# Last stage of a decoder: the second expert's down products and sums one slot later, values of two heads in one row strip

## The reference

```python
# cross attention, 16 heads of 8 features, 77 keys
scores = jnp.einsum('bhqd,bhkd->bhqk', Q, K) / math.sqrt(dk)
...
t = jnp.exp(log_t)[..., None]
attn = jax.nn.softmax(qk / (2.0 * t), axis=-1)
out = jnp.einsum('bhqk,bhkd->bhqd', attn, V)
x = x + _linear(out.transpose(0, 2, 1, 3).reshape(b, sq, d), Wo, bo)
# four experts, the best two of four weighted for each token
e0 = jax.nn.silu(x @ sw_w1) * (x @ sw_w3) @ sw_w2
e1 = jax.nn.gelu(sym @ me_c1w + me_c1b, approximate=False) @ me_c2w + me_c2b
...
h2 = _layer_norm(syn + attn, ce_n1g, ce_n1b)
ff = jax.nn.relu(h2 @ ce_f1w + ce_f1b) @ ce_f2w + ce_f2b
e2 = _layer_norm(h2 + ff, ce_n2g, ce_n2b) @ ce_gen_w + ce_gen_b
e3 = jax.nn.gelu(x @ ml_w1 + ml_b1, approximate=False) @ ml_w2 + ml_b2
```

## Time and profile before

| | us |
|---|---|
| median of 3 runs (lowest, highest) | 3040.72 (3040.23, 3042.76) |
| the profiled execution | 3037.89 |
| its span | 3036.1 |
| last stage, from about | 2066 |
| PE busy | 2738.4 |
| DVE busy | 2097.9 |
| ACT busy | 1920.1 |
| POOL busy | 1943.3 |

### The profile page before, as it was taken

The page is one execution under the profiler, slowest core; times in us unless marked ns, Lnnn a source line. Parts: engine busy times, 40 slices in busy tenths (PEclk is TensorE's granted clock), DMA queues, the critical chain, the costliest instruction groups (busy, mean ns, idle before and its releaser), DMA issues. The chain is left out here.

```text
span 3036.1 us, 83028 instructions
## 1 busy us (share of the span) xinstructions
PE 2738.4 (90%) x27974; PEld 2320.1 (76%) x27975; DVE 2097.9 (69%) x4496; ACT 1920.1 (63%) x4300; POOL 1943.3 (64%) x3244
## 2 busy tenths in 40 slices
PE   6999997999999999499997999995899999999996
PEld 5788776888888888388885888883677777777775
DVE  3677655667676766445555999997777878778543
ACT  3566553666666666355553777774878777787762
POOL 4456543456666666416667999984676777867652
PEclk9999997999999999699998999995899999999998
DMA  5566561000000000222222000000000000000000
GB/s 153 169 181 190 170 181 36 2 8 12 14 13 13 12 14 13 71 67 82 81 82 62 1 0 0 0 1 1 1 2 9 5 8 5 5 9 5 8 5 11
DMA packets 204792, 129.08 MB, mean 43 GB/s; under 512 B 13840, under 2 KB 197112, under 8 KB 203896
## 3 DMA queue, kind: packets, MB, share of 16 engines
q1 hardware_dynamic: 196344, 108.80, 12.0%
q0 software_dynamic: 8192, 16.79, 1.9%
HBM read 35.05 MB, written 90.51 MB: 41 GB/s over the span
## 5 line engine op out<-in xcount | busy, mean ns | idle before, releaser
L1552 PE MATMUL a_ps_s<-a_qk,w_ident 128*128 128x256 f32 x1024 | 238.5, 387 | 20.2 <-POOL a_qk L1659 19.1
L1007 POOL TENSOR_TENSOR x_p<-x_p,x_rz 128x1232 f32<-128x1232 f32 x64 | 143.9, 2248 | 165.6 <-DVE x_rz L1116 165.6
L584 DVE TENSOR_REDUCE a_nmax<-a_ps_s 128x4 f32<-128x512 f32 x256 | 164.9, 686 | 113.8 <-PE a_ps_s L373 113.7
L1659 POOL TENSOR_TENSOR a_qk<-a_qkv 128x2048 f32<-128x2048 f32 x64 | 235.6, 3681 | 2.6 <-POOL a_eight L218 1.0
L457 ACT ACTIVATE a_e<-a_ps_s 128x512 f32<-128x512 f32 x256 | 138.9, 595 | 152.8 <-PE a_ps_s L378 152.8
L1552 PEld LDWEIGHTS a_ps_s<-a_qk,w_ident 128*128 128x128 f32 x1024 | 192.0, 193 | 50.4 <-POOL a_qk L1659 22.7
L2374 POOL TENSOR_TENSOR x_sq<-x_e 128x1232 f32<-128x1232 f32 x64 | 143.2, 2238 | 126.2 <-DVE x_t_sq L2533 126.1
L1633 ACT ACTIVATE a_r<-a_o,w_a_rows 128x128 f32<-128x128 f32 x512 | 220.5, 521 | 1.6 <-DVE a_o L1718 1.6
L1387 POOL DMA_INDIRECT f_yg<-f_rows_out,f_index x120 | 114.9, 958 | 152.1 <-DVE f_yo L1467 134.4
L889 ACT ACTIVATE x_uu_hi<-x_ps_u 128x308 fp32r<-128x308 f32 x256 | 101.7, 423 | 106.0 <-PE x_ps_u L752 105.8
L1123 DVE TENSOR_REDUCE x_top<-x_ps_s 128x16 f32<-128x1232 f32 x64 | 91.2, 1424 | 111.2 <-PE x_ps_s L752 111.2
(11 more groups left out here) (626 smaller groups left out, 9742.0 us busy)
## 6 DMA issues: line engine op xcount, KB each, us to landing
f_rows_in<-a_zeros SPq DMA_DIRECT2D x31, 1088.0 KB, 5.4
f_rows_out<-a_zeros SPq DMA_DIRECT2D x31, 1088.0 KB, 8.8
f_xin<-f_rows_in SPq DMA_DIRECT2D x135, 64.0 KB
f_rows_out<-f_yo SPq DMA_DIRECT2D x135, 64.0 KB, 1.6
out<-x SPq DMA_DIRECT2D x16, 256.0 KB, 2.4
f_raw<-in_late_f SPq DMA_DIRECT2D x2, 1408.0 KB, 5.9
w_ctx<-in_ctx SPq DMA_DIRECT2D x1, 2464.0 KB
f_rows_in<-f_xr,f_where POOLq DMA_INDIRECT x128, 2.3
```

Source lines behind the costliest of these rows:

```text
L584: nc.vector.tensor_reduce(nmax[:, u % 2, g, :], ps_s[g][:, :].rearrange("p (t k) -> p t k", t=GROUP), AX.X, ALU.max, negate=True).then_inc ...
L1007: nc.gpsimd.tensor_tensor(wide, wide, rz[:, :].unsqueeze(2).broadcast_to([P, HEADS, K]), ALU.mult).then_inc(p_ready, 1)
L1552: ins = nc.tensor.matmul(ps_s[u % 2][:, 0:HEADS * HEADS], c.ident[:, :], qk[:, u % 2, k, :, :], start=k == 0, stop=k == HD - 1)
L1659: nc.gpsimd.tensor_tensor(qk[:, u % 2, :, :, :], qkv[:, u % UNROLL, 0, :, :].unsqueeze(3).broadcast_to(full), qkv[:, u % UNROLL, 1, :, :]. ...
```

## The change

1. `second` no longer holds b's down products. A new `third` issues them at place 1 of the gates' slot (THIRD = OPEN + 5), ahead of gate 0, and VectorE's `finished("b")` moves to place 1 of that slot. In `sums_of` b stands behind d and ahead of the `up` products. d's down products, one sequence of the tile each, stand at places 1, 4, 6 and 7 of SECOND instead of one at 4, two at 6 and one at 7.
2. v1 is 40 columns wide, zeros with the values in columns 8 to 15 and a one in column 24. Two heads use it with a window of 32 that begins at column 8 or 0, and their products are summed into one strip: rows 0 to 7 and 8 to 15 are the values, rows 16 and 24 the sums of the weights. ps_o then holds 256 columns, oz copies 256, two transposes turn them back, and the scaling is two instructions of 64 values.

```diff
-        v1 = sb("v1", [K, 2, HEADS, STRIP])
+        v1 = sb("v1", [K, 2, HEADS, WIDE])
...
             if (j := tile(t, SECOND)) is not None:
-                order += [("b", j, 0), ("d", j, 0)]
+                order += [("d", j, 0)]
+            if (j := tile(t, THIRD)) is not None:
+                order += [("b", j, 0)]
             if (j := tile(t, GATED)) is not None:
...
+                if n in (1, 4, 6, 7):
+                    downs("d", j, range(4), f["ml_2"], ((1, 4, 6, 7).index(n),))
+
+            def third(j, n):
+
                 if n == 1:
                     downs("b", j, (4, 5), f["c2"], range(T))
-                if n == 4:
-                    downs("d", j, range(4), f["ml_2"], (0,))
-                if n == 6:
-                    downs("d", j, range(4), f["ml_2"], (1, 2))
-                if n == 7:
-                    downs("d", j, range(4), f["ml_2"], (3,))
...
                         j, r = divmod(n, GROUPS)
+                        two, low = divmod(j, PAIR)
                         h = GROUP * r + j
-                        ins = nc.tensor.matmul(ps_o[strip(r), j * P:j * P + P], v1[:, s % 2, h, :], pT[:, h, :],
-                                               start=True, stop=True)
+                        ins = nc.tensor.matmul(ps_o[strip(r), two * P:two * P + P], v1[:, s % 2, h, HD - HD * low:WIDE - HD * low], pT[:, h, :],
+                                               start=low == 0, stop=low == PAIR - 1)
...
-                    for j in range(GROUP):
+                    for j in range(2):
                         ins = nc.tensor.transpose(ps_o[:, j * P:j * P + P], oz[:, j * P:j * P + P], c.ident[:, :])
...
-                    nc.scalar.activation(oz[:, :], ps_o[:, :], ACT.Copy).then_inc(oz_ready, 1)
+                    nc.scalar.activation(oz[:, :], ps_o[:, 0:2 * P], ACT.Copy).then_inc(oz_ready, 1)
...
-            nc.gpsimd.memset(v1[:, :, :, :], 1.0).then_inc(made, 1)
+            nc.gpsimd.memset(v1[:, :, :, :], 0.0).then_inc(pool_made, 1)
+            pool.wait_ge(pool_made, 3)
+            nc.gpsimd.memset(v1[:, :, :, 3 * HD:3 * HD + 1], 1.0).then_inc(made, 1)
...
-                if (j := tile(t, SECOND)) is not None and n == 1:
+                if (j := tile(t, THIRD)) is not None and n == 1:
                     finished("b", 1, j, "c2b")
...
-                    nc.vector.reciprocal(each, z[:, :, :, HD]).then_inc(rz_ready, 1)
+                    nc.vector.reciprocal(rz[:, :, :, :], z[:, :, :, 2 * HD::HD]).then_inc(rz_ready, 1)
...
+                    for n in range(2):
+                        ins = nc.vector.tensor_tensor(out[:, n, :, :, :], z[:, n, :, 0:2 * HD].rearrange("p g (j d) -> p g j d", d=HD),
+                                                      rz[:, n, :, :].unsqueeze(3).broadcast_to([P, GROUPS, PAIR, HD]), ALU.mult)
+                    ins.then_inc(o_ready, 1)
```

More of the change, by code:

```diff
@@ L1811, in cross_and_experts @@
         e, sq = sb("e", [P, 2, HEADS, K]), sb("sq", [P, HEADS, K])
-        v1 = sb("v1", [K, 2, HEADS, STRIP])
+        WIDE, PAIR = HD + STRIP, GROUP // 2
+        v1 = sb("v1", [K, 2, HEADS, WIDE])
         pT = sb("pT", [K, HEADS, P])
-        oz, rz, o = sb("oz", [P, 512]), sb("rz", [P, HEADS]), sb("o", [P, 2, D])
+        oz, rz, o = sb("oz", [P, 2 * P]), sb("rz", [P, PAIR, GROUPS, PAIR]), sb("o", [P, 2, D])
         t_max, t_z, t_sq = (sb(n, [P, 2, GRP, HEADS]) for n in ("t_max", "t_z", "t_sq"))
@@ L1883, in tile @@
             return (t - lag) // T if (t - lag) % T == 0 and 0 <= (t - lag) // T < TILES else None
-        OPENED, GATED, TURNED, MIXED, SECOND, TURNED2, CLOSED = (OPEN + n for n in (0, 1, 2, 3, 4, 6, 7))
+        OPENED, GATED, TURNED, MIXED, SECOND, THIRD, TURNED2, CLOSED = (OPEN + n for n in (0, 1, 2, 3, 4, 5, 6, 7))
         def gated(t):
@@ L2106, in experts @@
                     second(j, n)
+                if (j := tile(t, THIRD)) is not None:
+                    third(j, n)
                 if (j := tile(t, OPENED)) is not None:
@@ L2285, in _ @@
                     act.wait_ge(p_ps, t - PROJECT + 1)
-                    nc.scalar.activation(v1[:, spread % 2, :, 0:HD], ps_v.rearrange("p (h r) -> p h r", r=HD), ACT.Copy).then_inc(v_ready, 1)
+                    nc.scalar.activation(v1[:, spread % 2, :, HD:2 * HD], ps_v.rearrange("p (h r) -> p h r", r=HD), ACT.Copy).then_inc(v_ready, 1)
                 experts(t, 2)
@@ L2543, in _ @@
                     dve.wait_ge(z_ps, s + 1)
-                    z = ps_o[:, :].rearrange("p (j g r) -> p g j r", j=GROUP, g=GROUPS)
-                    each = rz[:, :].rearrange("p (g j) -> p g j", g=GROUPS)
-                    nc.vector.reciprocal(each, z[:, :, :, HD]).then_inc(rz_ready, 1)
+                    z = ps_o[:, 0:2 * P].rearrange("p (n g r) -> p n g r", n=2, g=GROUPS)
+                    nc.vector.reciprocal(rz[:, :, :, :], z[:, :, :, 2 * HD::HD]).then_inc(rz_ready, 1)
                     dve.wait_ge(rz_ready, s + 1)
                     wait(dve, oT_ps, s - 1)
-                    nc.vector.tensor_tensor(o[:, s % 2, :].rearrange("p (g j r) -> p g j r", g=GROUPS, j=GROUP), z[:, :, :, 0:HD],
-                                            each.unsqueeze(3).broadcast_to([P, GROUPS, GROUP, HD]), ALU.mult).then_inc(o_ready, 1)
+                    out = o[:, s % 2, :].rearrange("p (g n j d) -> p n g j d", g=GROUPS, n=2, j=PAIR)
+                    for n in range(2):
+                        ins = nc.vector.tensor_tensor(out[:, n, :, :, :], z[:, n, :, 0:2 * HD].rearrange("p g (j d) -> p g j d", d=HD),
+                                                      rz[:, n, :, :].unsqueeze(3).broadcast_to([P, GROUPS, PAIR, HD]), ALU.mult)
+                    ins.then_inc(o_ready, 1)
                 experts(t, 7)
```

## The result

The changed kernel took 3095.91 us (median of 4 runs, 3090.07 to 3099.68), the kernel before 3040.47 (4 runs, 3036.44 to 3042.76): 1.0183 times as long, 95% interval 1.0166 to 1.0199.

A forecast was written before the change was run, and what follows sets the result against it. VectorE's order in the gates' slot, not TensorE's amount of work, was taken to bound the kernel. 29.7 + 3 + 0.4 + 5.6 = +38.7 on the profiled 3037.9 gave 3076.6, with the median 2.8 above: 3079 us, range 3054 to 3098.

The forecast's parts named there:

- the forecast's own range: 3060 to 3090 us: a period at 2 to 3 us, clock at 0 to 10, end at its bounds; chance 0.70.
- SECOND loses nothing but its tail: SECOND: b's 1.79 us taken away were covered by ScalarE's chain; the router's operations start only 0.6 us earlier.
- The gates' slot: b's products wait for d's sum to free ps_d: stall 2.8 us, transposes of the weights +2.9 us, 0.6 already taken off.
- x: The forecast's new start of the router's operations on VectorE, 2519.80.
- 11 x (2.9 - 0.2) = +29.7: Eleven gates' slots with maximum and subtraction: 2.9 us lost in each, 0.2 given back by the pairing.
- The pairing: Two of four z transposes go; they pay only at the end of the TURNED slot: -0.2 us per four slots.
- The clock: Falls behind the 2.8 us stall cost 1.4 us each; bounds none and all 11, 0 to +15; four taken, +5.6.
- The rival with a fall in every gates' slot: Clock falls in every gates' slot: +15.4 for the clock, +48.5 in all, 3089 us; chance 0.13.
- The one of 2.16 cost nothing: Argument against the clock falling in every gates' slot: behind a 2.16 us stall at 2225.36 the granted clock stayed 1.00.
- The end: Last four slots, without maximum and subtraction: +1, +1, +2 and -1, so +3 us (ends -4 and +11).
- The faster rival: TensorE's amount of work decides: 128 transposes less at 0.11 us are 14.1 us, giving 3026.6; chance 0.07.
- the absorbed one: POOL's normalisation sets the gates' slot's end anyway, hiding TensorE's 2.7 us loss: only +3 and 0.4 stay, 3044 us; chance 0.05.

The follow-up runs named there:

- the kernel with fillers: Changed kernel plus 16 transposes into ps_o, ahead of the value products, where TensorE waits for d's sum in the gates' slot: 1.0104 of before.

## Why the prediction was right, point by point

Predicted 3079.0 in 3054 to 3098, slower at 0.87; measured 3095.91. The mechanism held; two sizes were off, in opposite directions. The measurement lies beyond the forecast's own range (3060 to 3090) and only 2 us inside the wide one: that it is inside at all owes something to luck, since no term stood for the largest error, the clock at the stage's end.

- **SECOND loses nothing but its tail.** The first 1.79 us were covered, as said: o's transpose still waits for ScalarE's v, now 0.98 us where it was 0.21. The way from there to the router's first operation took 7.22 us (2536.98 to 2544.20), before 8.05: 0.8 earlier, forecast 0.6. The difference is ScalarE's copy, 384 ns for 256 columns, so 0.2 less than the 596, in its one place on a chain.
- **The gates' slot.** Stall 2.37 us (said: 2.8); at full clock, in the kernel with fillers, up 0 at x + 7.43 (7.6) and the weights' transposes at x + 9.22 (9.35). From x to them were 5.83 us before, so +3.39, less 0.83 for the earlier router: +2.6, forecast +2.9. Of the slots it is 3.34 - 0.90 = +2.44, and TURNED and MIXED give back 0.34 (forecast 0.2). The term "11 x (2.9 - 0.2) = +29.7" measured 11 x 2.10 = **+23.1**.
- **The pairing.** -0.4 a group alone, forecast -0.2: it was not lost at MIXED's end, which gave 0.22. The two products of o take 0.36 us together against 0.29, and the memset of v with the small one behind it +0.4, as forecast.
- **The clock.** This is the step that failed: a fall at 1.4, "I take four, +5.6". The price was right (16.84 - 15.44 = 1.40), the number was not: nine of eleven gates' slots fell (all eleven with the move alone), and the clock was lower at the end and, in this execution, in the fill. Together some 13.8 + 11.6 + 3.9 = 29.3 us, far over the bound of 15 and the rival's 15.4, which counted the eleven steady slots alone. The rival with a fall in every gates' slot (3089) is the nearest to the measurement, and its reason was right. The forecast weighed one row with a fall against one without and took four of eleven. The row without one, 2.16 us at 2225.36, is the stall of slot 21, and it was the exception: behind the same stall the clock fell in ten of the twelve profiles. "The one of 2.16 cost nothing" was true of one execution. No run at hand then could tell; but one row on each side was no ground for a third of the slots, and the bound was the likelier value.
- **The end.** +3 was forecast with ends of -4 and +11; without falls of clock it is +6, with them +17.6. The saving of 0.9 to 2.7 that pre0 was to bring did not come: pre0 waits there for the turned x anyway (1.20 us for VectorE's x_m_lo at 3033.88).
- **The sum.** 0.4 + 23.1 + 6 + 29.3 = 58.8, against the 59.1 us of the last stage with its memset; forecast 38.7. The 2.7 us ahead of the stage are no part of the edit.

The faster rival (TensorE's work decides) and the absorbed one are excluded: TensorE has less work and the slot is 3.34 longer at full clock; and POOL, which might have hidden it, disappeared from the waits.

What stays open: where the 2.7 us ahead of the stage come from, what decides which slots keep their clock, and whether the pairing has a part in the late rise in slot 12. A second bank for b's products, which would part the two sums, was not tried; all eight are in use.

## What to carry over

When a product is moved, ask who holds its PSUM bank at the new place and who must free it: here one bank put two sums and two products in line, and a covered 1.8 us became 3.3 on the path. Price a new stall on TensorE twice, once for its length and once for the clock behind it, in every slot where it repeats and at the stage's end as well; and do not take a stall that kept its clock in one trace for a safe one. And when a chain lies on VectorE, look first for what the other engines do early that nobody needs yet: here the gain came only once POOL's ranks, wanted a slot later, were out of the way.

## What the runs showed of the hardware

- Behind the same stall of 2.37 us the clock fell from 2.4 to 1.2 GHz for a part of nine of the eleven gates' slots, and stayed in two; behind 2.33 us, with the move alone, it fell in eleven of eleven. With 1.35 us it fell in five of eleven, with 0.6 in none. One stall of 2.16 us, the same in twelve profiles, was followed by a fall in ten. When it begins drifts against the kernel: b's 16 passes took 3.61, 3.24, 2.85, 2.47 and 2.02 us in the gates' slots from 2371.68, 2429.30, 2486.91, 2544.52 and 2602.10, the last without a fall, yet each of the first four slots took 16.84, within 0.02. Sixteen transposes whose result is never used were worth 22 us. The Trainium skill (TensorE: Matmul & The Clock Gate, Part 1) says that idleness throttles the array: these kernels agree, as far as more of the stalls of 2.3 us than of those of 1.35 or 0.6 were followed by a fall.
- A VectorE sum of two 128x16 operands in SBUF took 2.00 us beside POOL's 2.25 us product, 0.17 without it. The Trainium skill (GPSIMD Engine Reference, Key points) says that GpSimd contends with VectorE instructions that have two inputs in SBUF; this run agrees with it, and here the wait lasts until POOL's instruction ends, at 2571.38.
